# Two instruction orders of VectorE and three waits of TensorE in a four-layer sequence kernel

## The reference

```python
x = layernorm(x + mamba2(x))            # layer 1: W_in, short convolution, state scan, gate, root mean square, W_out
# layer 2, "bounded": a product with ternary weights, its rows scaled by tanh(norm)/norm and a limit
out = (x @ weight) * scale
out = out * tanh(|out|) / |out|;  out = out * min(0.99 / |out|, 1)
x = layernorm(x + out)
# layer 3, recurrence (RG-LRU)
y    = gelu(x @ w_y + b_y)
conv = conv_b + sum_k conv_w[k] * shift(x @ w_x + b_x, 3 - k)
gx, ga = sigmoid(conv @ w_ig + b_ig), sigmoid(conv @ w_ag + b_ag)
a    = exp(-8 * ga * softplus(a_param));  mult = sqrt(1 - a * a)
h_t  = a_t * h_(t-1) + (gx * conv * mult)_t
x = layernorm(x + (h * y) @ w_out + b_out)
# layer 4, gated FFN; the weights are integer codes
Wg, Wu, Wd = (codes - 128) * scale[:, None]      # Wg, Wu: 2048 x 512, Wd: 512 x 2048
x = layernorm(x + (silu(x @ Wg.T) * (x @ Wu.T)) @ Wd.T)
```

## Time and profile before

| | us |
|---|---|
| median of 3 runs (1032.4 to 1034.07) | 1033.49 |
| the profiled execution | 1033.6 |
| its span | 1031.9 |
| TensorE busy | 999.0 |
| VectorE busy | 810.9 |
| ScalarE busy | 648.2 |
| GpSimd busy | 335.0 |

### The profile page before, as it was taken

How to read it: one execution, slowest core, us unless ns; L and a number is a source line. 1 busy time by engine, 2 the same in 40 slices (tenths; PEclk the granted TensorE clock), 3 DMA queues, 4 the chain that set the end, 5 groups by cost and what they waited for, 6 DMA issues and landing times. The chain is left out here.

```text
span 1031.9 us, 19678 instructions
## 1 busy us (share of the span) xinstructions
PE 999.0 (97%) x7402; PEld 832.3 (81%) x7402; DVE 810.9 (79%) x1429; ACT 648.2 (63%) x1339; POOL 335.0 (32%) x456
## 2 busy tenths in 40 slices
PE   6899999999999999999999999989999999999997
PEld 6789898999989887999999989975445875875873
DVE  5998999999999998876867776885858766766763
ACT  7968786867777685665566566666232761762750
POOL 2004334152414134425344443513421331331331
PEclk9999999999999999999999999999999999999999
DMA  7520313214040454501001102023601201101101
GB/s 231 205 99 33 131 63 99 104 58 149 13 156 6 139 173 166 215 1 42 19 27 42 43 1 84 32 101 102 225 1 63 61 2 63 62 2 51 32 1 62
DMA packets 44703, 81.38 MB, mean 79 GB/s; under 512 B 7360, under 2 KB 17600, under 8 KB 42560
## 3 DMA queue, kind: packets, MB, share of 16 engines
q1 hardware_dynamic: 44608, 80.11, 22.6%
HBM read 67.24 MB, written 12.85 MB: 78 GB/s over the span
## 5 line engine op out<-in xcount | busy, mean ns | idle before, releaser
L2311 PE MATMUL banks<-d_wd,d_hh 128*128 128x512 f16 x256 | 98.1, 383 | 2.1 <-DVE d_wd L2038 2.1
L2311 PE MATMUL banks<-d_wd,d_hl 128*128 128x512 f16 x256 | 98.0, 383 | 0.0
L650 DVE SCALAR_TENSOR_TENSOR a_xs<-a_xpre,a_cvec,a_xs 128x256 f32<-128x256 f32 x192 | 91.2, 543 | 0.4 <-ACT a_xs L453 0.4
L1887 POOL TENSOR_TENSOR d_hl<-d_h32s,d_hh 128x512 f16<-128x512 f32 x48 | 55.7, 1160 | 97.4 <-ACT d_hh L1982 97.4
L822 PE MATMUL banks<-a_xth,a_wgh 128*128 128x256 f32 x256 | 74.3, 290 | 1.7 <-DVE a_wgl L592 1.7
L675 DVE TENSOR_TENSOR_SCAN a_L<-a_L,a_ident 128x512 f32<-128x512 f32 x64 | 74.8, 1212 | 0.5
L822 PE MATMUL banks<-a_xth,a_wxh 128*128 128x256 f32 x256 | 74.6, 291 | 0.0
L822 PE MATMUL banks<-a_xtl,a_wxh 128*128 128x256 f32 x256 | 72.5, 283 | 0.0
L822 PE MATMUL banks<-a_xth,a_wxl 128*128 128x256 f32 x256 | 72.4, 283 | 0.0
L822 PE MATMUL banks<-a_xtl,a_wgh 128*128 128x256 f32 x256 | 72.2, 282 | 0.0
L822 PE MATMUL banks<-a_xth,a_wgl 128*128 128x256 f32 x256 | 72.2, 282 | 0.0
(11 more groups left out here) (361 smaller groups left out, 3338.9 us busy)
## 6 DMA issues: line engine op xcount, KB each, us to landing
a_L<-decays SPq DMA_DIRECT2D x16, 1024.0 KB, 4.8
a_xf<-in_x_turned SPq DMA_DIRECT2D x16, 256.0 KB, 3.8
a_xr<-in_x SPq DMA_DIRECT2D x16, 256.0 KB, 2.7
tokens<-a_xr SPq DMA_DIRECT2D x16, 256.0 KB, 2.0
c_xb<-tokens SPq DMA_DIRECT2D x16, 256.0 KB, 2.7
d_xin<-tokens SPq DMA_DIRECT2D x16, 256.0 KB, 4.2
d_r<-tokens SPq DMA_DIRECT2D x16, 256.0 KB, 2.7
d_wd_codes<-in_down_w SPq DMA_DIRECT2D x4, 1024.0 KB, 9.3
```

The costliest lines, as they stand in the source:

```text
L650: ins = dve.scalar_tensor_tensor(out=out, in0=xpre[:, m, k:k + T], scalar=cvec[:, m, k:k + 1], in1=out, op0=ALU.mult, op1=ALU.add)
L1887: pool.tensor_tensor(hl[:, m, :], (h32s[:, m % 4, :] if i else h32[:, m % 2, :]), hh[:, m, :], ALU.subtract).then_inc(s_hl, 1)
L2311: ins = pe.matmul(ps_o[:, c % 2, :], h[:, m, cols(c)], wd[:, m, :], start=(m == 0 and h is hh), stop=(m == M - 1 and h is hl), skip_group_ ...
```

## The change

1. In the recurrence's VectorE program `scaled(s + 1)` is called ahead of `low_hy(s - 1)` in steps 1 to 6; it came behind it.
2. In step 6 two of the four conversions are issued behind `squared(6)` instead of ahead of it.
3. `output(s)` for s = 6 takes the form that only s = 7 had: both token groups' products with c_hyh first, then a wait for c_hyl, then the products with c_hyl.
4. The wait for the last mean square moves from ahead of the first projection of step 0 to between its halves, behind the transposes `turn_in(1)`.
5. In the FFN's chunk 0, for m = 7, 8 and 9, sums of weights and the product come ahead of the two conversions; the conversions were first.
6. The wait for all pieces of d_wd ahead of `down(0, 0)` is replaced by one wait per pair of row blocks inside it.

```diff
--- before.py
+++ after.py
@@ -1474,13 +1474,13 @@
             for s in range(NS):
                 if s:
                     recur(s - 1)
+                    if s + 1 < NS:
+                        scaled(s + 1)
                     low_hy(s - 1)
                 if s == 0:
                     convolve(s)
                     scaled(s + 1)
                 else:
-                    if s + 1 < NS:
-                        scaled(s + 1)
                     convolve(s)
                 low_conv(s)
                 if s == 0:
@@ -1497,7 +1497,7 @@
                     before["low_piece"]()
                 if s == NS - 2:
                     following_stage["low_rows"]()
-                    for i in range(4):
+                    for i in range(2):
                         following_stage["convert"](i)
                 if s + 2 < NS:
                     turn_in(s + 2)
@@ -1506,6 +1506,9 @@
                     for i in range(4, 8):
                         following_stage["convert"](i)
                 squared(s)
+                if s == NS - 2:
+                    for i in range(2, 4):
+                        following_stage["convert"](i)
                 if s == 1:
                     following_stage["peak_of_scales"]()
                 if s == 3:
@@ -1578,7 +1581,7 @@
                 done.then_inc(arrived, 1)
 
         def output(s):
-            if s + 1 == NS:
+            if s + 2 >= NS:
                 pe.wait_ge(s_hyh, s + 1)
                 pe.wait_ge(s_ssq, C * NS)
                 for j in range(C):
@@ -1598,16 +1601,19 @@
                 pe.wait_ge(s_ssq, C * (s + 2) + j + 1 if s + 2 < NS else C * NS)
                 tokens(ps_o[:, j, :], hyh, hyl, W["out"], j).then_inc(s_out, 1)
 
+        def after_sums(then):
+            then(1)
+            pe.wait_ge(*last["mean_sq"])
+
         def main(following_stage):
             for s in range(NS):
                 if s == 0:
                     pe.wait_ge(s_xh, C)
                     pe.wait_ge(*split["x"])
-                    pe.wait_ge(*last["mean_sq"])
                 else:
                     pe.wait_ge(s_xl, C * s + C)
                 project(ps_a, W["x"], xth, xtl, lambda q: wait(pe, s_ga, M * (s - 1) + 2 * q + 2), s_xb,
-                        None if s else (s_xl, C), None if s else lambda: turn_in(1))
+                        None if s else (s_xl, C), None if s else lambda: after_sums(turn_in))
                 if s + 1 < NS:
                     bounded(s + 1)
                 if s == 0:
@@ -2177,12 +2183,12 @@
                 if i:
                     combined(i)
                 for m in range(early, M if i == 0 else 0):
+                    for op, j in {9: ((0, 0),), 11: ((1, 0), (0, 2)), 13: ((1, 2),), 14: ((0, 4),)}.get(m, ()):
+                        weight_sums(op, j)
+                    product(i, m)
                     if 7 <= m < 10:
                         convert(2 * m - 4)
                         convert(2 * m - 3)
-                    for op, j in {9: ((0, 0),), 11: ((1, 0), (0, 2)), 13: ((1, 2),), 14: ((0, 4),)}.get(m, ()):
-                        weight_sums(op, j)
-                    product(i, m)
                     if m >= 12:
                         convert(M + 2 * m - 24)
                         convert(M + 2 * m - 23)
@@ -2307,6 +2313,8 @@
             for m in ms:
                 if c == 0:
                     pe.wait_ge(s_hl, M * i + m + 1)
+                    if i == 0 and m % 2 == 0:
+                        pe.wait_ge(s_prep_down, m // 2 + 1)
                 for h in (hh, hl):
                     ins = pe.matmul(ps_o[:, c % 2, :], h[:, m, cols(c)], wd[:, m, :],
                                     start=(m == 0 and h is hh), stop=(m == M - 1 and h is hl), skip_group_check=True)
@@ -2320,7 +2328,6 @@
                         gate_up(i, m)
                         if m == M - 2:
                             front(i + 1, (0, 1))
-                    pe.wait_ge(s_prep_down, len(pieces) - M)
                     down(i, 0)
                 else:
                     combined(i)
```

## The result

| | us |
|---|---|
| before, median of 4 runs | 1033.04 |
| after, median of 4 runs (1022.2 to 1023.27) | 1022.56 |
| ratio | 0.9899, 95% interval 0.9881 to 0.9916 |
| profiled execution of after, its span | 1023.27, 1021.5 |

What follows compares the result with a forecast made beforehand. TensorE bounds the kernel, busy 97% of the span, so gains are its waits and lower-clock time. 1.1 + 2.9 + 1.9 + 0.9 + 2.1 + 1.7 = 10.6 us off 1033.6 gives 1023.0 us, range 1020.0 to 1027.5.

Steps and rivals of the forecast that it cites:

- Entry: Entry into the recurrence: moving the mean-square wait gains 1.1 us, limited by VectorE's idle stretch; bounds 0 and 1.16.
- Rival 1: The clock falls in a new place, behind a longer c_cvh wait in step 0; costs up to 1.7 us; chance 0.14.
- Rows scaled ahead: Recurrence: scaling before low halves makes TensorE the only bound in steps 1 to 5; 2.9 us, bounds 0 and 3.2.
- 5 x 0.58: Steps 1 to 5: TensorE's 0.58 us of waiting for c_cvh and c_cvl, read in step 3, saved in each; 2.9 us.
- Rival 3: Steps 1 to 5: another wait, such as c_hyl, replaces c_cvh; half or none of the 2.9 us kept; chance 0.06.
- Steps 6 and 7: Moved conversions and two-part output let recur start at 672.0 against 673.87; 1.9 us, bounds 1.3 and 2.9.
- VectorE comes to the conversions 1.1 us earlier: Step 6: the earlier scaling brings VectorE to the conversions at 663.6, the first two ending by 664.9.
- rival 2: GpSimd and VectorE block each other per instruction, delaying squared and product 11; 0.6 + 0.9 us less gain; chance 0.10.
- First chunk, products: FFN's first chunk: product 7 ahead of conversions removes its wait, but gate_up 13 takes part back; 0.9 us, bounds 0 and 1.4.
- product 11 ends at about 746.8 in either order: FFN's first chunk: VectorE's work ahead of product 11 keeps the same sum, so 0.9 of 1.4 us stay.
- d_wd wait: Before down 0: waiting per pair of row blocks removes the whole wait for d_wd pieces; 2.1 us.
- clock: Behind the d_wd wait at down 0: the fall to the lower clock goes with the wait; 1.7 us.

Runs made afterwards that it cites:

- x3: Changed kernel with the two-part output of step 6 undone, so that output waits for c_hyl at its start; 1022.35 us, ratio 0.9895.
- x8: Changed kernel with the wait for the last mean square put back ahead of the first projection; 1024.18 us, ratio 0.9899.
- x7: Kernel before, plus nine 512-column products that nobody reads ahead of its wait for d_wd; 1033.67 us against 1034.78, ratio 0.9991.
- x4: Changed kernel with the low halves put back ahead of the scaled rows; 1026.26 us, ratio 0.9935.
- x1: Kernel before with only the rows scaled ahead of the low halves; 1028.23 us against 1033.29, ratio 0.9954.
- x2: Changed kernel with all four conversions back ahead of the square and the output of step 6 whole again; 1021.97 us, ratio 0.9892.
- x9: Changed kernel with step 6's output whole again and conversions 2 and 3 moved on into step 7, ahead of 4 to 7; 1020.97 us, ratio 0.9884.
- x6: Changed kernel with the conversions put back ahead of products 7 to 9 in the FFN's first chunk; 1023.9 us, ratio 0.9891.
- x5: Changed kernel with one wait for all d_wd pieces put back ahead of down 0; 1026.07 us, ratio 0.9908.
- x10: x9 plus w_ig's low half moved behind step 0's low rows and the mixer's last normalisation behind c_cv(0)'s rounding; 1024.78 us, ratio 0.9915.

## Why the prediction was right, point by point

**Entry: 1.1 forecast, 1.07 measured.** The limit was read rightly: VectorE gained its one idle stretch of 1.16 and no more. TensorE gave the rest back in one of two ways. In x3 it did so as forecast, by a wait of 1.82 us for c_cvh. In after and six more traces it worked at the lower clock behind transposes and one-column products and waited 0.25 to 0.74 us. The forecast took the clock to fall because of the a_rs wait; in these seven traces that wait is gone and the clock falls at the same place, so that wait isn't needed for the fall, and what decides it stays open. The figure is also luckier than it looks: against the 23.80 and 24.16 that this stretch took in x8 and x7 the gain would be some 2 us.

**Rival 1 (the clock falls in a new place) is real.** It needs a trace in which the clock doesn't fall earlier, and x3 is one: behind the 1.82 us wait it falls and takes 1.49 us. The rival's price was 1.7 "less whatever TensorE would soon wait for anyway", and that left 0.25 us. In how many runs of after this happens isn't known.

**Rows scaled ahead: 2.9 forecast, 3.44 measured**, 3.28 by x4 and 3.39 by x1. The mechanism is shown by x1 and x4. The failed step, small as it is, is "5 x 0.58". The 0.58 was read in step 3, and step 3 (from c_wig product to c_wig product) gave 0.58; steps 1, 2, 4 and 5 gave 0.75, 0.72, 0.69 and 0.59, and step 6, which the term left out, 0.11 (each good to 0.1). One step's surplus was taken for all. The total lies over the upper bound of 3.2. Rival 3 (another link holds the step) is out: the groups are 0.48 apart.

**Steps 6 and 7: 1.9 forecast, 2.01 measured, the cause half wrong.** `recur` starts at 668.99. TensorE's step 6 starts 2.90 us earlier in this trace (655.14 against 658.04), so on the old time that is 671.89, against 672.0 forecast. Two misses cancel in this: `squared` ended at 669.66 on the old time and not at 669.1, and the two moved conversions took 2.23 us and not 2.9, as the second met nothing (0.68). The cause is half wrong too, for x2 and x4 show how the gain divides: edit 1 alone gives 2.3, edits 2 and 3 alone 1.2, both 2.0. The failed step is "VectorE comes to the conversions 1.1 us earlier" without asking what that does to the old order. It moves the second and third conversion out of GpSimd's reach, and that is as good as the edit meant to do it. And the moved conversions stand between `squared` and `recur`, where 2.23 us are longer than the 1.13 that the root leaves free; x9 takes them out and gains 1.06 more.

**The lock rule (rival 2).** `squared`, with two float32 inputs, took 1.21 alone, 1.76 beside GpSimd in after and 2.31 in x2. The first of the two c_xb additions by itself, in after and then in x2:

```profile
664.38 1.30 POOL L1198 TENSOR_TENSOR c_xb<-c_xb,c_bo 128x512 f32<-128x512 f32 x1
...
663.60 1.73 POOL L1198 TENSOR_TENSOR c_xb<-c_xb,c_bo 128x512 f32<-128x512 f32 x1
```

It ends at 665.68 and 665.33, and `squared` ends 1.08 us behind it in both (666.76, 666.41), about its own 1.21: it waited for that one addition to the end. This is what the Trainium skill states in SBUF — State Buffer, section "Who interferes with whom": a VectorE instruction with two SBUF inputs contends with GpSimd's reads; the trace agrees. So the rival's mechanism is real. Its price in after was 0.55 for `squared`, made good by the conversions as said above, and none for product 11, where the rival had 0.6 + 0.9.

**First chunk, products: 0.9 forecast, 1.41 measured** (x6). The failed step is "product 11 ends at about 746.8 in either order". From the end of L1447 to its start VectorE took 746.04 - 730.90 = 15.14 us before and 740.26 - 725.99 = 14.27 after. Two rows make up 0.83 of these 0.87 us: an idle 0.17 ahead of product 10 is gone, and the first conversion takes 0.98 instead of 1.64. That conversion ends 0.55 behind GpSimd's pair of d_hl rows in both orders (732.46 against 731.91 before, 727.55 against 727.00 after). Product 7, which isn't held (0.74 in either order), now runs in the time that the conversion spent waiting. The forecast took the sum of VectorE's times to be the same in any order, and it isn't where GpSimd holds one of them. TensorE began gate_up 13 at 741.76, 0.8 behind the end of product 11, and so found it ready.

**d_wd wait: 2.1 forecast, 2.26 measured; clock: 1.7 forecast, 1.71 measured.** x5 brings both back; x7 brings back the clock alone.

**The sum.** 10.6 was forecast, the parts gave 11.9, the medians 10.5. Two terms were 0.5 us too small (rows scaled ahead, products of the first chunk), and those of the entry and of steps 6 and 7 came out partly by luck. That 10.6 and 10.5 are so close is luck as well: the parts add up to 1.3 us more than was forecast, and the medians hold 1.4 less than the parts, for a reason that no run here shows.

## What to carry to other kernels

Where an engine's start-to-start distances exceed their unheld pace, look for a wait that no idle time shows; here, swapping two VectorE instructions so that one runs while VectorE waits for ScalarE's answer gave that surplus back in every step. Before adding an edit for a stall, work out what the other edits do to it: here one swap had already removed all that two more were for. When an instruction is moved, follow its store as well, and all that stands behind that on the DMA queue, and look at what the other engine has to do beside its new place (x10). Don't add up an engine's times as if they were the same in any order: a row that was held by GpSimd gets shorter when something that isn't held goes ahead of it.

## What the runs showed of the hardware

- The clock fell to its lower level behind an idle wait of 2.1 us on TensorE (0.79 over 8 us, 1.7 us lost: before and x5), behind one of 1.82 (0.60 over 4 us, x3) and one of 3.24 (0.61 over 4 us, x10), and not behind one of 2.9. With the 2.1 us filled by products that nobody reads (x7) it stayed at 1.00.
- Behind transposes and sixteen one-column products it also fell with no wait longer than 0.34 us near (after, 0.79 over 8 us), and in one trace with the same instructions it didn't (x3, 1.00).
- VectorE's int32 to float16 conversion of 128x1024 takes 0.69 us alone and 0.98 to 2.90 beside GpSimd's two-input rows. In four such rows it ended 0.55 or 0.56 us behind the row that held it, however early it had come: 664.18 against 663.63 (x2), 668.22 against 667.66 (before), 668.46 against 667.91 and 727.55 against 727.00 (after).
- Two traces of one kernel's unchanged first layer differ by up to 2 us, while most later stretches repeat to 0.1 us. Read single edits from stretches, totals from medians.
